# Graph attention and three hops of relational attention on one core: state loads spread over the pipeline's drain, and five smaller edits

## The reference

```python
h = relu(layernorm(x))
# layer 0: graph attention, 2 heads of 64
feat = h @ W;  el = sum(feat*attn_l);  er = sum(feat*attn_r)      # per node and head
e = leaky_relu(el[src] + er[dst], 0.2)
alpha = softmax of e over the edges with the same dst
x = x + layernorm(segment_sum(feat[src]*alpha, dst) + bias) * gamma + beta
# layer 1: three hops, head = src, tail = dst, rel = edge_emb[edge_type]
agg = entity = relu(layernorm(x)); out = 0
for _ in range(3):
    att = sum((agg[head] @ q_w) * tanh((rel * agg[tail]) @ k_w))
    w = softmax of att over the edges with the same head
    agg = segment_sum(w * rel * agg[tail], head) / max(count, 1)
    agg = agg / max(norm(agg), 1e-12)
    out = out + agg + entity
x = x + out
```

## Time and profile before

| | us |
|---|---|
| Runs of before: median, lowest, highest | 9809.44, 9801.89, 9814.32 |
| Profiled execution's own time | 9807.02 |
| Its span, first to last instruction | 9805.2 |
| Layer 0 pass: first and last row gather of POOL | 831.81, 2976.39 |
| Hop passes: first row gather of each | 3094.03, 5332.33, 7565.02 |
| Hop passes: last row gather of each | 5250.66, 7487.29, 9723.54 |
| PE busy, over the span | 8923.7 (91%) |
| DVE, ACT, POOL busy | 7921.7, 7321.4, 6810.7 (81%, 75%, 69%) |

### The profile page before, as it was taken

How to read it: one execution, slowest core, us unless ns; L and a number is a source line. 1 busy time by engine, 2 the same in 40 slices (tenths; PEclk the granted TensorE clock), 3 DMA queues, 4 the chain that set the end, 5 groups by cost and what they waited for, 6 DMA issues and landing times.

```text
span 9805.2 us, 277571 instructions
## 1 busy us (share of the span) xinstructions
PE 8923.7 (91%) x65693; PEld 7235.6 (74%) x65693; DVE 7921.7 (81%) x33650; ACT 7321.4 (75%) x23591; POOL 6810.7 (69%) x7059
## 2 busy tenths in 40 slices
PE   7996777777776999999997999999997999999997
PEld 6985666666664777777775777777775777777775
DVE  7898999999997777777775777777775777777775
ACT  2204999999996777777775777777775777777775
POOL 1336777777775777777775777777775777777775
PEclk9998999999997999999998999999998999999998
DMA  2003444444444555555556555555556555555556
GB/s 49 5 12 82 108 109 109 109 109 109 109 109 115 159 159 159 159 159 158 159 159 133 158 160 160 157 159 159 159 159 140 159 159 159 159 159 159 159 159 122
DMA packets 1133743, 1308.57 MB, mean 133 GB/s; under 512 B 452629, under 2 KB 847723, under 8 KB 1133325
## 3 DMA queue, kind: packets, MB, share of 16 engines
q1 hardware_dynamic: 899446, 841.26, 28.0%
q0 software_dynamic: 229008, 460.45, 21.1%
q10 hardware_dynamic: 5126, 4.76, 0.2%
HBM read 1041.61 MB, written 260.45 MB: 133 GB/s over the span
## 4 chain that ended last, share of the span: by engine, by line
PE 63%; DMA 10%; DVE 9%; issue 8%; POOL 7%; ACT 3%; SPq 1%; DVEq 0%; POOLq 0%; ACTq 0%
PE bank L737 52%; DMA agg<-agg_d,arena 6%; POOL agg L705 6%; PE bank L897 5%; PE bank L882 5%; PE bank L850 2%; DMA agg<-feat_d,arena 2%; DVE agg L1545 2%; DVE agg L1555 2%; ACT arena L1011 2%; DVE arena L1535 1%; POOL wide L718 1%; DMA arena<-type_d 1%; DVE arena L1513 1%; DVE arena L1504 0%
## 5 line engine op out<-in xcount | busy, mean ns | idle before, releaser
L705 POOL DMA_INDIRECT agg<-agg_d,arena x5124 | 4852.1, 947 | 1731.1 <-issue 1432.1
L1655 DVE TENSOR_TENSOR arena<-agg,bank 128x256 f32<-128x256 f32 x2562 | 1080.2, 422 | 1451.1 <-PE bank L737 1064.4
L705 POOL DMA_INDIRECT agg<-feat_d,arena x1708 | 1618.3, 947 | 529.4 <-issue 421.4
L737 PE MATMUL bank<-arena 128*128 128x129 f32 x10248 | 1825.6, 300 | 32.6 <-ACT arena L1090 30.5
L737 PE MATMUL bank<-tmp,wide 128*128 128x256 f32 x5124 | 1540.1, 383 | 10.1 <-DMA wide<-left_d 10.1
L737 PE MATMUL bank<-tmp,kw_s 128*128 128x256 f32 x5124 | 1532.9, 381 | 0.0
L737 PEld LDWEIGHTS bank<-arena 128*128 128x128 f32 x10248 | 1338.5, 190 | 211.3 <-issue 43.3
L1086 ACT ACTIVATE arena<-arena 128x1 f32<-128x1 f32 x2562 | 754.6, 295 | 931.7 <-DVE arena L1519 890.6
L1081 ACT ACTIVATE arena<-agg,arena 128x256 f32<-128x256 f32 x2562 | 1337.9, 522 | 57.8 <-DVE arena L1648 52.2
L1094 ACT ACTIVATE tmp<-bank 128x256 f32<-128x256 f32 x2562 | 982.1, 383 | 427.6 <-PE bank L737 372.6
L1648 DVE CUSTOM_DVE_ANT_0 agg<-bank,arena 128x256 f32<-128x256 f32 x2562 | 1228.6, 480 | 19.6 <-issue 8.0
(11 more groups left out here) (242 smaller groups left out, 17251.0 us busy)
## 6 DMA issues: line engine op xcount, KB each, us to landing
state_d<-arena SPq DMA_DIRECT2D x488, 455.0 KB, 2.7
arena<-key_d SPq DMA_DIRECT2D x489, 448.0 KB
arena<-type_d SPq DMA_DIRECT2D x367, 448.0 KB
wide<-left_d SPq DMA_DIRECT2D x2562, 64.0 KB
agg<-agg_d,arena POOLq DMA_INDIRECT x5124
agg<-feat_d,arena POOLq DMA_INDIRECT x1708
arena<-er_d SPq DMA_DIRECT2D x854, 1.0 KB
arena<-peers SPq DMA_DIRECT2D x489, 7.0 KB
```

The lines of the kernel that those rows point to most:

```text
L705: nc.gpsimd.indirect_dma_start(out=rows_r[:, k % R, c, 0:width], out_offset=None, in_=table, in_offset=bass.IndirectOffsetOnAxis(ap=peer_r ...
L737: return nc.tensor.matmul(out, lhsT, rhs, start=start, stop=stop)
L1655: V.tensor_tensor(val_r[:, j % R, :, 0:F], rows_r[:, j % R, :, 0:F], bank[0][:, 0:G].rearrange("p (c f) -> p c f", c=2), ALU.mult).then_in ...
```

## The change

- Parts become 18, 17, 7 and 7 blocks. The states of the first three are loaded by SP and POOL during the drain, as soon as the stores that can hold them have landed; only the last part waits for every store. ACT loads two blocks of the last part. SP's loads stand between its last stores, and the `left` ring moves to a place in `wide` behind the first 35 blocks. The tail of `state_d` is written once with finite numbers.
- In a hop's border DVE computes two parts' lengths before the first directions, and adds to `xs` after all four; ACT squares in that order too and has a first `Sqrt` right after the first square. SP stores the four parts of `agg` and then four parts of `left` (16, 16, 8 and 9 blocks). POOL restarts with `aggT_ready` 4 and `xs_done` 1 instead of 6 and 2.
- In the prologue POOL gathers the edges by target before it scatters the tails; DVE decodes them before the last three steps of the plan; ACT sends the window list out before the plan is whole. DVE no longer waits for `meta_stored[1]`; SP waits for it behind layer 0's pass and ACT ahead of it.
- The rings' first values: one slot of `acc_r`, one of `min_r` and one column of `val_r` instead of all.
- `beta` is added to `xs` in 13 pieces of up to 4 blocks in chunks 40 to 52 of the sort.
- `emb_low` has 128 rows, the lower 64 zero, and its matmul reads all 128 rows of the one-hot.

```diff
-PARTS = ((0, 12), (12, 24), (24, 36), (36, NB))
-ACT_LOADS = (range(0, 4), range(12, 16), range(0), range(0))
-POOL_LOADS = (range(4, 8), range(16, 20), range(24, 30), range(36, 42))
-SP_LOADS = (range(8, 12), range(20, 24), range(30, 36), range(42, NB))
-TILES_OF = (range(0, 3), range(3, 6), range(6, 9), range(9, LB))
+EARLY = 35
+PARTS = ((0, 18), (18, EARLY), (EARLY, 42), (42, NB))
+POOL_LOADS = (range(0, 8), range(18, 26), range(35, 39), range(42, 44))
+SP_LOADS = (range(8, 18), range(26, 35), range(39, 42), range(44, 47))
+SP_FIRST = 2
+ACT_LOADS = range(47, NB)
+TILES_OF = (range(0, 4), range(4, 8), range(8, 10), range(10, LB))
+LEFTS = ((0, 16), (16, 32), (32, 40), (40, NB))
...
+            sp.wait_ge(rowid_made, 1)
+            for at in range(0, U * SW, NG):
+                n = min(NG, U * SW - at)
+                sp.dma_start(state_d[:, (NG - U) * SW + at:(NG - U) * SW + at + n], giota[:, 0:n]).then_inc(tail_finite, 16)
...
+                    if b.last and k == 0:
+                        for i in range(2):
+                            sp.wait_ge(q["stored"][i], b.landed("stored", i * R - 3 * U))
+                        load_states(layer, 0, SP_LOADS[0])
+                        for i in range(2):
+                            sp.wait_ge(q["stored"][i], b.landed("stored", i * R - 2 * U))
+                        load_states(layer, 1, SP_LOADS[1][0:SP_FIRST])
+                    if b.last and k == STORE[layer] - R:
+                        load_states(layer, 1, SP_LOADS[1][SP_FIRST:])
+                        sp.wait_ge(q["stored"][0], b.landed("stored", -U))
+                        apart(sp)
+                        if layer == 1:
+                            sp.wait_ge(q["scores_ready"], b.count(-1))
+                        load_states(layer, 2, SP_LOADS[2])
...
-            pool.wait_ge(tails_known, 1)
-            nc.gpsimd.indirect_dma_start(
-                out=sorted_edges[1], out_offset=bass.IndirectOffsetOnAxis(ap=tail_at[:, 0:1], axis=0),
-                in_=zeros[:], in_offset=None).then_inc(tails_stored, 16)
             for s in range(2):
-                pool.wait_ge(windows_in[s], 16)
                 if s == 0:
+                    pool.wait_ge(windows_in[0], 16)
                     pool.wait_ge(feat_stored, 32)
                 else:
+                    pool.wait_ge(tails_known, 1)
+                    nc.gpsimd.indirect_dma_start(
+                        out=sorted_edges[1], out_offset=bass.IndirectOffsetOnAxis(ap=tail_at[:, 0:1], axis=0),
+                        in_=zeros[:], in_offset=None).then_inc(tails_stored, 16)
+                    pool.wait_ge(windows_in[1], 16)
...
                 for part in range(4):
+                    stored(((BODIES - 2, BODIES - 2), (BODIES - 1, BODIES - 1), (BODIES, BODIES - 1), (BODIES, BODIES))[part])
+                    if part == 2 and layer == 1:
+                        pool.wait_ge(pipes[1]["scores_ready"], pool.snap(h * NG + NG))
...
-                        last = mm(bank[0][:, c * P:(c + 1) * P], hot_r[0:RELS, j % R, c * P:(c + 1) * P], emb_low[:], False, True)
+                        last = mm(bank[0][:, c * P:(c + 1) * P], hot_r[:, j % R, c * P:(c + 1) * P], emb_low[:], False, True)
...
                 square_of(0)
+                nc.scalar.activation(root_junk[:], rowid[:, 0:1], ACT.Sqrt)
+                square_of(1)
+                load_states(1, hop)
                 length_of(0)
-                square_of(1)
+                length_of(1)
+                square_of(2)
+                square_of(3)
...
+            def add_beta(n):
+                lo = 4 * (n - BETA_AT)
+                if 0 <= lo < NB:
+                    hi = min(lo + 4, NB)
+                    V.tensor_tensor(xs[:, lo:hi, :], xs[:, lo:hi, :],
+                                    beta_s[:].rearrange("p (o f) -> p o f", o=1).to_broadcast([P, hi - lo, F]), ALU.add)
...
-                    do(V.memset(acc_r, 0.0))
-                    do(V.memset(min_r, 0.0))
-                    do(V.memset(val_r, 1.0))
+                    do(V.memset(acc_r[:, U - 1:U, :], 0.0))
+                    do(V.memset(min_r[:, R - 1:R, :], 0.0))
+                    do(V.memset(val_r[:, :, :, F:F + 1], 1.0))
...
+            decode(0)
+            plan_keep(1)
+            plan_limits(1)
+            plan_targets(1)
+            turn_peers(0)
+            decode(1)
+            turn_peers(1)
...
                 lengths(0)
+                lengths(1)
                 directions(0)
-                for part in range(1, 4):
-                    lengths(part)
-                    add_hop(part - 1)
-                    directions(part)
-                add_hop(3)
+                lengths(2)
+                directions(1)
+                lengths(3)
+                directions(2)
+                directions(3)
+                for part in range(4):
+                    add_hop(part)
```

More of the change, by code:

```diff
@@ L60 @@
 SIGNS_AT, TOTALS_AT = 12, 68
+BETA_AT = 40
 TABLES_AT = (84, 88, 92, 96)
+PART_WORDS = 18 * F
+assert PARTS[0][1] - 1 - NB < -2 * U and PARTS[1][1] - 1 - NB < -U and PARTS[2][1] - 1 - NB < -R
 SW = F + 2
@@ L181, in gnn_kernel @@
         emb_pair = sb("emb_pair", [2 * RELS, F], BF16)
[L182 removed]
+        emb_low = sb("emb_low", [2 * RELS, F], BF16)
         rel_row = sb("rel_row", [2 * RELS, 1])
@@ L432, in _ @@
             sp.dma_start(key_d[0].rearrange("(l w) -> l w", l=LANES), s_key).then_inc(sorted_stored, 16)
-            for i in range(2):
-                sp.wait_ge(meta_stored[i], 16)
+            sp.wait_ge(meta_stored[0], 16)
             sp.wait_ge(sorted_stored, 16)
@@ L492, in first_unit, with load_states @@
                 sp.dma_start(flat(type_r), type_d[0:R * G].partition_broadcast(P)).then_inc(d, 16)
-            def load_states(layer):
+            def load_states(layer, part, blocks):
                 apart(sp)
-                for part in range(4):
-                    for b in SP_LOADS[part]:
-                        g = sp.value_load(lastg[layer][0:1, b:b + 1], min_val=0, max_val=NG - 1)
-                        sp.dma_start(wide[:, b * SW:(b + 1) * SW], state_d[:, bass.ds(g * SW, SW)]).then_inc(state_in[part], 16)
+                for b in blocks:
+                    g = sp.value_load(lastg[layer][0:1, b:b + 1], min_val=0, max_val=NG - 1)
+                    sp.dma_start(wide[:, b * SW:(b + 1) * SW], state_d[:, bass.ds(g * SW, SW)]).then_inc(state_in[part], 16)
+            sp.wait_ge(tail_finite, 3 * 16)
             sp.dma_start(peer_r[:, 0:R, :].rearrange("p a b -> p (a b)"), peers[0][:, 0:2 * R]).then_inc(peers_loaded[0], 16)
@@ L503, in _ @@
             sp.wait_ge(sorted_stored, 3 * 16)
+            sp.wait_ge(meta_stored[1], 16)
             first_unit()
@@ L520, in store_left @@
                 def store_left(part):
-                    lo, hi = PARTS[part]
+                    lo, hi = LEFTS[part]
                     sp.wait_ge(left_copied, tiles + TILES_OF[part].stop)
@@ L711, in gather_states, with stored @@
             def gather_states(layer, h):
-                for i in range(2):
-                    pool.wait_ge(pipes[layer]["stored"][i], 16 * BODIES if h is None else pool.snap(h * (16 * BODIES) + 16 * BODIES))
-                apart(pool)
+                def stored(bodies):
+                    for i in range(2):
+                        pool.wait_ge(pipes[layer]["stored"][i], 16 * bodies[i] if h is None else pool.snap(h * (16 * BODIES) + 16 * bodies[i]))
+                    apart(pool)
                 for part in range(4):
+                    stored(((BODIES - 2, BODIES - 2), (BODIES - 1, BODIES - 1), (BODIES, BODIES - 1), (BODIES, BODIES))[part])
+                    if part == 2 and layer == 1:
+                        pool.wait_ge(pipes[1]["scores_ready"], pool.snap(h * NG + NG))
+                        apart(pool)
                     for b in POOL_LOADS[part]:
@@ L911, in lefts @@
                     if t < LB:
-                        if t % 3 == 0 and t < 12:
-                            pe.wait_ge(agg_ready, parts + (t // 3 + 1))
-                            apart(pe)
+                        for part in range(4):
+                            if t == TILES_OF[part].start:
+                                pe.wait_ge(agg_ready, parts + (part + 1))
+                                apart(pe)
                         if t >= 2:
@@ L985, in load_states @@
                 apart(act)
-                for part in range(4):
-                    for b in ACT_LOADS[part]:
-                        g = act.value_load(lastg[layer][0:1, b:b + 1], min_val=0, max_val=NG - 1)
-                        act.dma_start(wide[:, b * SW:(b + 1) * SW], state_d[:, bass.ds(g * SW, SW)]).then_inc(state_in[part], 16)
+                for b in ACT_LOADS:
+                    g = act.value_load(lastg[layer][0:1, b:b + 1], min_val=0, max_val=NG - 1)
```

(7 more changed lines are left out.)

56 lines of the change are left out of this document (29 added, 27 removed).

## The result

| | before | after | forecast |
|---|---|---|---|
| Median of the runs, us | 9805.22 (6 runs) | 9761.52 (6 runs) | 9720 |
| Profiled execution's own time and span | 9807.02, 9805.2 | 9773.91, 9772.1 | 9717 |
| First row gather of layer 0 | 831.8 | 836.8 | 828.1 |
| Pass of layer 0, first to last row gather | 2144.6 | 2151.0 | 2144.6 |
| Hop passes | 2156.6, 2155.0, 2158.5 | 2163.7, 2163.0, 2165.8 | as before |

The ratio after to before is 0.9958, 95% interval 0.9948 to 0.9968: a real gain of 0.4%, half of the forecast and 4.5 us outside its range of 9700 to 9757.

What follows compares the result with a forecast made beforehand. The prediction took POOL's row gathers to bound the passes, so only borders could shrink: 3.7 + 10 + 58 + 18 = 89.7 us off the profiled 9807.02 gave 9717, set at 9720 us for the median, range 9700 to 9757.

Steps and rivals of the forecast that it cites:

- POOL as the bound: All passes: POOL's two row gathers per group, 2.50 us, set the pace, with PE almost as long at 2.48.
- Rival (b): Hop passes: PE is the bound, so its shorter groups give up to 871 us more, 8849 us; chance 0.02.
- in the passes this saves nothing: Passes: emb_low of 128 rows cuts PE's group from 2.48 to 2.14 us, but POOL's 2.50 us hides it.
- of which I keep 1.4: Drain's end of a hop: PE's faster last 7 groups finish 2.4 us earlier, 1.4 kept as SP is then later.
- Rival (e): Relation products: 128-row weight loads overlap nothing, PE's group stays 2.48 us, time 9724 us; chance 0.05.
- Prologue, 3.7 us: Ahead of layer 0's pass: tail scatter behind target gathers and plan steps behind the decode save 3.7 us, between 0 and 6.
- beta in the sort, nothing: Sort: adding beta in pieces fills DVE's 0.61 us wait per chunk for PE, costing nothing, at worst 13 × 0.2.
- Behind layer 0, 10 us: Border after layer 0's pass: early state loads and the shorter store bring POOL's first gather 10 us earlier, 5 to 14.
- Hop borders, 29 us each: Two borders between hops: loads in the drain and reordered DVE work save 29 us each, 58 in all, each between 22 and 33.
- rival (c): Hop borders: they shrink half as much, the last store 10 to 20 us late, time 9745 to 9780; chance 0.20.
- Behind hop 2, 18 us: Last gather to end: earlier additions and all output written in one go save 18 us, 14 to 21.
- (d), slower: Drain: filler groups reading row 0 choke DMA, SP's early loads delay each hop's last store, time 9895 us; chance 0.03.

Runs made afterwards that it cites:

- e2: The kernel before with only emb_low of 128 rows added: 9810.82 us, ratio 1.0008 to before.
- e16: The changed kernel with DVE's two 16-bit masks of a hop written by an instruction with two tensor inputs: 9960.02 us, ratio 1.0160 to before.
- e3: The changed kernel with filler groups at a hop's end gathering 256 different rows instead of row 0: 9690.62 us, ratio 0.9886 to before.
- e14: The kernel before with filler groups gathering 256 different rows instead of row 0: 9713.95 us, ratio 0.9909 to before.

## Why the forecast was wrong, point by point

- **POOL as the bound:** right. Rival (b) is refuted by e2, and e16 shows that the gathers' lengths add up to the pass. But "1.25 us" was taken as POOL's own constant. It is 1.249 where nothing holds a gather up, and how many are held up depends on where DVE's masks fall. "All four passes stand at 2135 us" also passed over 20 us in each hop, which before's own rows had (2155.0 to 2158.5): mostly POOL's stop of 14.7 to 16.6 us over the filler groups.
- **emb_low, "in the passes this saves nothing":** the step that failed, at 17.5 of the 46 missing us. PE's side was right (the steps are 0.05 and 0.06, and a group is 4003.24 − 4001.21 = 2.03 us there). But the edit cost 17.5 us, since twice as many gathers start just behind a mask and are held up, 3.6 ns in the mean of all. The 2.4 us at each drain's end were right as DVE's time; "of which I keep 1.4" failed, as SP was later by more than that and hid them all. Rival (e), PE not sped up, didn't happen.
- **Prologue, 3.7 us:** the wrong sign, −2.4: 6.1 us. "Target gathers start at 785.74" took the tail scatter's place in a row for its cost; 0.4 of it was on the path. "The three plan steps lie in DVE's wait" overlooked what is queued behind them, the turned peers of layer 0, and that their store then meets the load of those peers.
- **beta in the sort, nothing:** right. From scatter 39 to 53 the sort takes 77.19 us in the kernel before and in after alike. That the tail of `state_d` and the first values cost nothing fits too, but was not tried alone.
- **Behind layer 0, 10 us:** right; 107.7, and 106.3 to 107.0 in the other executions, against 115.8 to 117.7.
- **Hop borders, 29 us each:** 24.8 and 19.6, from 81.7 and 77.7 to 56.9 and 58.1, so 13.6 are missing. Behind the landing of the last store the border is as laid out (23.3 against 22.2). Ahead of it: "SP is there just in time" failed, since its first 12 loads stand in DMA that the filler groups choke, 1.75 instead of 1.06 us each. The last store lands 33.7 and 34.8 us behind the last gather, 3.9 and 5.0 us later than the 29.8 of the layout; and the layout took the first border for both, though in the second the store had landed at 28.0. That is rival (c) in kind, but at less than the 10 to 20 us a hop that it named; without the loss in the passes the time would not have reached its 9745 to 9780.
- **Behind hop 2, 18 us:** 12.5, from 81.7 to 69.1, so 5.5 are missing. The last store lands 33.4 us behind the last gather instead of 30.1, which is 3.3 of them; the output itself took 14.5 us against 11.6 + 2.7.
- In sum 17.5 + 6.1 + 13.6 + 5.5 = 42.7 of the 46 us that are missing (89.7 − 43.7). The rest is no more than the two medians of before differ by (9809.44 from three runs, 9805.22 from six).
- **(d), slower:** didn't happen, though its fear was right: e3 and e14 show that choke at work, at 1.75 us a load in the drain.

## What to carry to other kernels

A paced engine's interval isn't a constant: where GpSimd issues gathers back to back, a VectorE instruction like these masks can hold one up, and an edit that speeds up a third engine can change how often the two meet. Ask of a moved step what stands behind it on its own engine and what its DMA will meet, and measure a gap from the event ahead of it, not by the instruction that happens to be in it. Take a border's length from all its instances. Pad gathers with different rows, not with one, and then look again at what ends last: here it was the late store with one row, and POOL's own state gathers with many.

## What the runs showed of the hardware that was not expected

- 128 rows of one gather that all read the same 512 bytes choke all DMA: 89 GB/s at a DMA share of 1.05, which is all engines busy, beside 177 GB/s at 0.60 for as many gathers of different rows. With 256 different rows in the last groups of a hop the kernel before is 86 us faster and the changed one 71. SP's loads of 3.7 us each in the earlier trace rows and the 96 GB/s of the earlier trace rows were that.
- A DVE mask of 0.28 us holds up a row gather by 0.07 us if the gather starts 0.05 to 0.10 us behind the mask's start; one of 0.48 us by 0.28.
- 128-row weights are cheaper for PE than 64-row ones between 128-row neighbours: 0.055 us a step instead of 0.16.
